# One transformer layer on one core: parts stored one by one, K's and Q's later parts at other places in a chunk, a third score bank in the last chunks

## The reference

```
x = L0_attn_hidden_states                       # (4, 512, 512) float32
x = x + attn(layernorm(x), w_attn, b_attn, w_proj, b_proj)
x = x + ffn(layernorm(x), w_gate, w_up, w_down)

attn: qkv = h @ w_attn + b_attn                 # 32 heads of 16
      scores = q k^T / 16 + slope[h] * (j - i)  # causal
      out = softmax(scores) v;  out @ w_proj + b_proj
ffn:  (silu(h w_gate^T) * (h w_up^T)) w_down^T  # inner width 1376
```

## Time and profile before

| | |
|---|---|
| median of 3 runs | 832.5 us (829.67 to 833.55) |
| the profiled execution | 831.38 us, of which the span is 829.7 |
| PE busy | 782.1 us, 94% |
| DVE, ACT, POOL busy | 643.4, 417.5, 298.7 us |
| mean granted clock of PE | 0.996 |

### The profile page before, as it was taken

The page is one execution under the profiler, slowest core; times in us unless marked ns, Lnnn a source line. Parts: engine busy times, 40 slices in busy tenths (PEclk is TensorE's granted clock), DMA queues, the critical chain, the costliest instruction groups (busy, mean ns, idle before and its releaser), DMA issues.

```text
span 829.7 us, 13389 instructions
## 1 busy us (share of the span) xinstructions
PE 782.1 (94%) x4554; PEld 542.7 (65%) x4554; DVE 643.4 (78%) x1608; ACT 417.5 (50%) x796; POOL 298.7 (36%) x437
## 2 busy tenths in 40 slices
PE   3899899999999999999998899999999999999998
PEld 2655455556555565555554477888878878888886
DVE  6498887878888888977887156849999787888773
ACT  4335666665666566565657524334346434334431
POOL 6223334342443434423434403324441043443342
PEclk9999999999999999999999999999999999999999
DMA  8873656656574565747563416051225321121052
GB/s 285 213 240 111 188 171 197 196 154 204 173 244 140 172 206 181 231 129 218 187 189 130 160 68 217 0 174 43 77 63 179 127 105 66 71 77 52 13 165 101
DMA packets 75372, 122.80 MB, mean 148 GB/s; under 512 B 13075, under 2 KB 38342, under 8 KB 75305
## 3 DMA queue, kind: packets, MB, share of 16 engines
q1 hardware_dynamic: 74217, 121.69, 46.2%
q10 hardware_dynamic: 1088, 0.26, 0.1%
HBM read 79.34 MB, written 42.32 MB: 147 GB/s over the span
## 4 chain that ended last, share of the span: by engine, by line
PE 69%; DVE 13%; DMA 7%; ACT 4%; issue 3%; POOL 2%; SPq 2%; ACTq 0%; DVEq 0%
PE bank L1280 25%; PE bank L1933 12%; PE bank L1199 7%; PE bank L1126 6%; PE bank L1111 5%; PE bank L1182 5%; PE bank L1158 5%; DVE bank L919 4%; DMA pv_dram<-weighed 2%; PE bank L1115 2%; ACT pt L751 2%; POOL scratch L650 1%; DVE scratch L891 1%; DMA row_sums<-pv_dram 1%; DVE mx L917 1%
## 5 line engine op out<-in xcount | busy, mean ns | idle before, releaser
L751 ACT ACTIVATE pt<-bank 128x512 f32<-128x512 f32 (+1 forms) x384 | 196.7, 530 | 124.2 <-PE bank L1182 121.8
L919 DVE CUSTOM_DVE_ANT_0 bank<-bank,mask_qk 128x512 f32<-128x512 f32 (+3 forms) x416 | 195.8, 512 | 42.5 <-PE bank L1158 41.1
L1182 PE MATMUL bank<-q_st,k_st 116*128 116x512 bf16 (+3 forms) x512 | 132.2, 301 | 12.0 <-ACT pt L751 10.6
L1158 PE MATMUL bank<-k_st,q_st 97*128 97x512 bf16 (+3 forms) x512 | 132.8, 306 | 9.5 <-DMA q_st<-slopes_dram 5.4
L1520 POOL TENSOR_TENSOR wd_lo<-wd_raw,wd_hi 128x512 fp32r<-128x512 f32 x34 | 45.7, 1351 | 152.6 <-ACT wd_hi L1552 152.6
L656 POOL TENSOR_SCALAR_AFFINE_SELECT pt<-pt 128x256 f32<-128x256 f32 x128 | 56.1, 438 | 119.8 <-ACT pt L751 119.8
L1158 PEld LDWEIGHTS bank<-k_st,q_st 97*128 97x128 bf16 x512 | 42.0, 98 | 73.2 <-issue 39.5
L660 POOL TENSOR_SCALAR_AFFINE_SELECT pt<-pt 128x256 f32<-128x256 f32 x128 | 54.0, 422 | 78.5 <-ACT pt L751 78.3
L1199 PE MATMUL bank<-pt,v_nat 128*32 128x512 f32 (+3 forms) x1024 | 77.0, 442 | 3.1 <-POOL pt L656 2.3
L1182 PEld LDWEIGHTS bank<-q_st,k_st 116*128 116x128 bf16 x512 | 45.8, 98 | 42.2 <-ACT pt L751 20.7
L1933 PE MATMUL bank<-wd_hi,w_hi 128*128 128x512 f32 x176 | 69.8, 397 | 2.1 <-issue 1.9
(11 more groups left out here) (186 smaller groups left out, 1712.0 us busy)
## 6 DMA issues: line engine op xcount, KB each, us to landing
stack_dram<-scratch SPq DMA_DIRECT2D x32, 384.0 KB, 3.1
q_st<-stack_dram SPq DMA_DIRECT2D x32, 384.0 KB
k_st<-stack_dram SPq DMA_DIRECT2D x32, 384.0 KB
wd_raw<-w_down SPq DMA_DIRECT2D x44, 256.0 KB, 3.4
xt<-w_gate_up SPq DMA_DIRECT2D x20, 512.0 KB, 3.6
stack_dram<-scratch SPq DMA_DIRECT2D x32, 256.0 KB, 3.7
pv_dram<-weighed SPq DMA_DIRECT2D x32, 256.0 KB, 4.5
weighed<-pv_dram SPq DMA_DIRECT2D x17, 256.0 KB
```

The costliest lines, as they stand in the source:

```text
L751: act.activation(pt[:, h % PT_RING, COL0[k]:COL0[k] + WIDE[k]], bank[3 + (3 * h + k) % 2][:, 0:WIDE[k]], ACT.Exp, scale=1.0 / HD).then_inc ...
L919: last = dve.tensor_tensor_reduce(bank[k][:, at:at + n], bank[k][:, at:at + n], mask_qk[:, S - n:S], 1.0, NEG, ALU.add, ALU.max, mx[:, h % ...
L1158: last = pe.matmul(bank[k][:, at:at + n], q_st[0:K_MAX, s, h % 4, t * P:(t + 1) * P], k_st[0:K_MAX, s, h % 4, 0:n], start=True, stop=not b ...
L1182: last = pe.matmul(bank[3 + u % 2][:, at:at + n], k_st[0:K_EXP, s, h % 4, t * P:(t + 1) * P], q_st[0:K_EXP, s, h % 4, t * P:S], start=True ...
```

## The change: part by part

1. `store_parts` issues one DMA as each part is made, each broadcast to the rows that use it (3, 2 and 1 rows; the six rows stand in another order), and waits for `act_read`, `p2_done` and `p3_done` in turn.
2. `load_stacks` issues the slopes' DMA first, ahead of the waits for the stored parts.
3. In SP's loop `store_pv` and the load of the row sums go ahead of the stores of K, except in cb 5.
4. On ACT `second_part` of Q goes behind the second exponential of the last head, and an `attention_hi` of that place behind the third. `second_part` of K moves from head 0 to head 1, except in cb 5; there DVE takes K's remainder ahead of the chunk's first scores.
5. On POOL `clear_future` is cut in two, and a third part goes between its two masks: Q's at head 3, K's at head 1 (in cb 5 ahead of head 0).
6. `weigh_values` waits for the last second mask ahead of its third pass, not its second.
7. From head 114 on the shifted scores use three banks in turn (5, 3, 4).
8. The twelve projection matmuls of chunks 30 and 31 are laid two by two over heads 1 to 3, and all of `weight_lo` is in chunk 30.

```diff
@@ -33,5 +33,4 @@
 
-Q_TERM = (0, 1, 2, 0, 1, 0)
-K_TERM = (0, 0, 0, 1, 1, 2)
-TERMS = len(Q_TERM)
+PART_ROWS = ((slice(2, 5), slice(1, 6, 4), slice(0, 1)), (slice(0, 3), slice(3, 6, 2), slice(4, 5)))
+TERMS = 6
 ROW_X = TERMS * HD
@@ -129,2 +128,10 @@
 
+THREE_FROM = 3 * (HEADS - 14)
+
+
+def shifted_bank(u):
+
+    return 3 + u % 2 if u < THREE_FROM else (5, 3, 4)[(u - THREE_FROM) % 3]
+
+
 def masked_by_tensor(h):
@@ -415,2 +422,6 @@
 
+        def k_at(c):
+
+            return 0 if c % CB == 5 else 1
+
         def late(c):
@@ -494,8 +505,11 @@
                 c, n = "QK".index(kind), group_made(b, g)
-                q_parts, k_parts = part[:, 0, :, :], part[:, 1, :, :]
-                sources = ((q_parts[:, 0:3, :], q_parts[:, 0:2, :], q_parts[:, 0:1, :]),
-                           [k_parts[:, i:i + 1, :].broadcast_to([P, m, S]) for i, m in enumerate((3, 2, 1))])
-                sp.wait_ge(p3_done, 2 * n + c + 1)
-                for r, m, src in zip((0, 3, 5), (3, 2, 1), sources[c]):
-                    sp.dma_start(stack_dram[c, b * G + g, r:r + m].rearrange("r p s -> p r s"), src).then_inc(parts_stored[c], 16)
+                for i in range(3):
+                    if i == 0:
+                        sp.wait_ge(act_read, act_reads(kind, b, g))
+                    if i == 1:
+                        sp.wait_ge(p2_done, 2 * n + c + 1)
+                    if i == 2:
+                        sp.wait_ge(p3_done, 2 * n + c + 1)
+                    sp.dma_start(stack_dram[c, b * G + g, PART_ROWS[c][i]].rearrange("r p s -> p r s"),
+                                 part[:, c, i:i + 1, :].broadcast_to([P, 3 - i, S])).then_inc(parts_stored[c], 16)
 
@@ -505,2 +519,4 @@
                 n = group_made(a // G, a % G)
+                h = 4 * c % H
+                sp.dma_start(q_st[ROW_X:K_SUM:2, s, :, :], slopes_dram[:, h:h + 4, :]).then_inc(stacked[s], 16)
                 for i, st in enumerate((q_st, k_st)):
@@ -509,4 +525,2 @@
                                  [:, at:at + 4, :]).then_inc(stacked[s], 16)
-                h = 4 * c % H
-                sp.dma_start(q_st[ROW_X:K_SUM:2, s, :, :], slopes_dram[:, h:h + 4, :]).then_inc(stacked[s], 16)
 
@@ -577,2 +591,6 @@
                     load_group(loaded_at(c))
+                if c > 0 and cb != 5:
+                    store_pv(c - 1)
+                if sums_of(c) is not None:
+                    load_row_sums(sums_of(c))
                 for kind, mb, i in made(c - 1)[1:]:
@@ -582,6 +600,4 @@
                     load_stacks(c + 3)
-                if c > 0:
+                if cb == 5:
                     store_pv(c - 1)
-                if sums_of(c) is not None:
-                    load_row_sums(sums_of(c))
                 if cb == 3 and b > 0:
@@ -651,3 +667,3 @@
 
-            def clear_future(h):
+            def clear_first(h):
                 head = pt[:, h % PT_RING, :]
@@ -657,2 +673,5 @@
                                    pattern=[[0, 2], [1, P]], channel_multiplier=-1).then_inc(masked, 1)
+
+            def clear_second(h):
+                head = pt[:, h % PT_RING, :]
                 pool.wait_ge(exp_done, 3 * h + 3)
@@ -682,7 +701,8 @@
                 for i in range(4):
-                    if i == 3:
-                        for kind, mb, g in made(c)[:1]:
-                            if kind == "Q":
+                    if i == 0 and k_at(c) == 0:
+                        for kind, mb, g in made(c - 1)[1:]:
+                            if kind == "K":
                                 third_part(kind, mb, g)
-                    if i == 0:
+                    clear_first(4 * c + i)
+                    if i == 1 and k_at(c) == 1:
                         for kind, mb, g in made(c - 1)[1:]:
@@ -690,3 +710,7 @@
                                 third_part(kind, mb, g)
-                    clear_future(4 * c + i)
+                    if i == 3:
+                        for kind, mb, g in made(c)[:1]:
+                            if kind == "Q":
+                                third_part(kind, mb, g)
+                    clear_second(4 * c + i)
                     if i == 3 and statistics_at(c) is not None:
@@ -750,3 +774,3 @@
                 act.wait_ge(t_done, 3 * h + k + 1)
-                act.activation(pt[:, h % PT_RING, COL0[k]:COL0[k] + WIDE[k]], bank[3 + (3 * h + k) % 2][:, 0:WIDE[k]],
+                act.activation(pt[:, h % PT_RING, COL0[k]:COL0[k] + WIDE[k]], bank[shifted_bank(3 * h + k)][:, 0:WIDE[k]],
                                ACT.Exp, scale=1.0 / HD).then_inc(exp_done, 1)
@@ -815,2 +839,4 @@
                     exponential(h, 0)
+                    exponential(h, 1)
+                    held = False
                     if i == 3:
@@ -819,4 +845,4 @@
                                 second_part(*tile)
-                    exponential(h, 1)
-                    if i == 0:
+                                held = True
+                    if i == k_at(c):
                         for tile in made(c - 1)[1:]:
@@ -824,5 +850,7 @@
                                 second_part(*tile)
-                    if highs(c, i) is not None:
+                    if highs(c, i) is not None and not held:
                         attention_hi(*highs(c, i))
                     exponential(h, 2)
+                    if highs(c, i) is not None and held:
+                        attention_hi(*highs(c, i))
                     if tokens_at(c, i) is not None:
@@ -1017,2 +1045,5 @@
 
+                    if i == 0 and k_at(c) == 0:
+                        for tile in made(c - 1)[1:]:
+                            read_tile(*tile)
                     scored(0)
@@ -1032,3 +1063,3 @@
                         for tile in made(c - 1)[1:]:
-                            if (tile[0], tile[2]) != ("P", 3):
+                            if k_at(c) == 1 and (tile[0], tile[2]) != ("P", 3):
                                 read_tile(*tile)
@@ -1054,4 +1085,5 @@
                         normalise_tokens(normalised_at(c), i)
-                    if c in (CHUNKS - 3, CHUNKS - 2):
-                        weight_lo(2 * (c - CHUNKS + 3) + i // 2, i % 2)
+                    if c == CHUNKS - 2:
+                        weight_lo(i, 0)
+                        weight_lo(i, 1)
 
@@ -1135,3 +1167,3 @@
                     k = c - (CHUNKS - 2)
-                    for p in range(lo, min(hi, 3 * TT)):
+                    for p in range(lo // 2, hi // 2):
                         project("P", B - 1, p // 3, 3 * k + p % 3, 3 * k + p % 3 + 1)
@@ -1177,3 +1209,5 @@
                 u = 3 * h + k
-                need(pe, exp_done, u - 1)
+                if u == THREE_FROM:
+                    pe.wait_ge(dve_read, dve_reads("P", B - 2, 2))
+                need(pe, exp_done, u - 1 if u < THREE_FROM else u - 2)
                 for t in T_TILES[k][::-1]:
@@ -1181,3 +1215,3 @@
                     at = S - P if t == 3 else 0
-                    last = pe.matmul(bank[3 + u % 2][:, at:at + n], k_st[0:K_EXP, s, h % 4, t * P:(t + 1) * P],
+                    last = pe.matmul(bank[shifted_bank(u)][:, at:at + n], k_st[0:K_EXP, s, h % 4, t * P:(t + 1) * P],
                                      q_st[0:K_EXP, s, h % 4, t * P:S], start=True, stop=True)
@@ -1192,3 +1226,3 @@
                         pe.wait_ge(m_copied, min(c + 2, CHUNKS))
-                    if t == 1:
+                    if t == 3:
                         pe.wait_ge(masked, 8 * c + 8)
```

6 lines of the change are left out of this document (3 added, 3 removed).

## The result

The changed kernel takes 812.39 us in the median of 6 runs (811.54 to 816.73), the kernel before 831.28 in the same set of runs (6 runs, 827.98 to 833.55): ratio 0.977, 95% interval 0.973 to 0.980. The forecast was 812, in a range of 804 to 824. A later set of runs gave 812.6 and a ratio of 0.974 (0.970 to 0.978). The size is right. Not all of its terms are, and the runs show that the parts of the gain depend on each other in a way that I had not written.

A forecast was written before the change was run, and what follows sets the result against it. PE was taken to bound the kernel, busy for 782.1 us of the span. 831.4 - 13 (middle) - 3 (ahead of the chunks) - 4 (tail) = 811.4; the median lies 1.1 above that execution, so 812, range 804 to 824.

The forecast's parts named there:

- Prologue, 3 us: Ahead of the chunks: stores issued as parts are made, slopes first, shorten PE's first wait; 3 us, bounds 1.3 and 4.4.
- Middle, 13 us: Q/K chunks: the new order removes PE's waits, 1.0 us at each of 13 chunks; bounds 6.5 and 17.8.
- The 1.37 us a Q/K chunk: Time each of a batch's four Q/K chunks was said to lose beyond PE's own pace, about 1.37 us.
- DVE as a brake on chunk 13: Chunk 13: DVE, busy 14.02 of 14.58 us, delays Q's remainder; of the 2 us lost there, 1.0 was left.
- costs nothing: Q/K chunks: K's second part a head later was said to cost nothing while ACT has idle time.
- counted above: SP's order: storing weighed values ahead of K's stores removes DVE's 2.22 us wait, already included in the 13 us.
- thin value: Chunk 13: early stores land K's stack 2 us earlier against a wait of 0.74; cover thin, as PE comes earlier too.
- The late wait: In weigh_values at Q/K chunk ends: waiting for the second mask before the third pass is covered, 0.6 us to spare.
- Tail, 4 us: Last chunks, 29 to 31: third bank, spread projections and moved weight_lo gain 4 us; bounds 1 and 6.
- DVE takes over: Rival: waits for ACT become waits for DVE's maxima or remainder, half the middle term stays; 820 us, chance 0.2.
- Slower: Rival: the last second mask comes too late behind Q's third part and weigh_values stops halfway; 838 us, chance 0.03.
- The clock: Rival: PE's clock falls in the last chunks, the tail gives 1 us or nothing; 815 to 816 us, chance 0.1.

The follow-up runs named there:

- the maxima first: Changed kernel plus one wait: in chunk 29 SP issues the two division loads only after the small DMA of chunk 30's maxima has landed; 812.7 us, ratio 0.979.
- the tail undone: Changed kernel with two score banks to the end, projection matmuls in blocks of four, and weight_lo in chunks 29 and 30 as before; 815.7 us, ratio 0.978.

## Why the prediction was right, and where it was not

**Prologue, 3 us: nothing.** The step that failed is the time that the last store needs to land. The last store does leave 0.03 us behind the third part instead of 0.96. But it took 4.3 to 5.75 us to land in the ten traces with the new order, 3.35 to 5.3 in the four with the old one; my bounds were 3.1 and 4.5. From the end of the third part to the landing that is 5.0 us on average against 5.3. I had called the time to land "not shown with so little ahead of it", but little lies ahead of it only in SP's order: in the changed kernel's trace the two stores ahead of it, issued at 25.87 and 26.99, land at 30.13 and 31.82, and the DMA engines are full from 22.5 to 28.2 us (a share of 1.06). The weights have no part in this; in each trace they had all landed before the first store of parts left. The 2.0 us that the prediction took from the Trainium skill ("DMA: Bandwidth & Descriptors", section "Anatomy of one DMA") stand there for DMAs that GpSimd issues. These come from SP, and none of the 14 landed in under 3.35 us. PE still waits 2.10 us, and the clock still falls (0.73 over the stretch of the earlier trace rows). Chunk 0 started at 52.5 to 55.8 us in the first group and at 51.9 to 55.6 in the second: the third part itself ends anywhere from 27.2 to 30.3 us, so a gain of 0.3 can't be seen.

**Middle, 13 us: 16.4.** The mechanism at the end of a Q/K chunk is as I read it from the earlier trace rows: the last heads of cb 1 and 7 took 3.68 us and now take 2.98, and Q's order undone brings the 3.68 back. (The 1.37 us a Q/K chunk was a mean; by the prediction's own numbers it is 5.3 / 4 = 1.32. The last head of cb 4 gains only 0.18, those of cb 5 up to 1.39.) DVE as a brake on chunk 13 was the mis-sized term: I left it 1.0 us of 2. It took 0.3 in the first trace and nothing in the second, though DVE is full, and chunks 5 and 21 reach 12.53 as well. With that, batches 1 and 2 gained 4.4 us each for my 4.0; batch 0 gained 5.7, 0.85 of it in chunk 3, a chunk with P and T where I had counted none.

**What carries it** I had wrong, and that the total came near is in part luck. I put the 13 us on Q's order, wrote that K's part a head later "costs nothing", that SP's order was "counted above", and gave the early stores thin value. Undone one by one, these four (Q's order, K's place, SP's order, the stores) are worth 11.7, 5.4, 5.7 and 9.7 us: 32.5 for a gain of 16.4. Q's order without the other three makes the middle 6.6 us longer than before (380.4 us); the other three without it gain 4.2 (369.6). Both of these kernels also have the rows' places and the slopes' early DMA. I had the rows for it: each time I measured a DMA against PE as it then ran (a wait of 0.74 us; the earlier trace rows), and did not move the deadline by the 1.37 us a Q/K chunk that I was about to give PE. K's place was the same fault: ACT had idle time over a chunk, but the part stands ahead of the copy on which the transpose one head later depends, and ACT's idle time was in waiting for DVE's remainder ahead of it.

**The late wait** I had costed within the 13 us. It is worth 0.4 to 0.6 us there, and some 0.6 to 1.0 in the last chunk, where I had not counted it.

**Tail, 4 us: 1.8 in one trace, 3.8 in the other.** Over the twelve traces with the new tail it is 3.1 to 4.2 in the nine whose clock stayed up, and 1.6 to 2.4 in the three whose clock fell. Of the 3.8, 0.4 fell in chunk 28, where I had nothing, 0.6 in chunk 29, where I had 1.3 (with the maxima first it was 1.2), and 2.8 in chunks 30 and 31, where I had 3.6 less 0.9 for the clock. In the first trace chunk 29 lost 0.3, and the last two won 1.6. With three banks the clock is 1.00 in every chunk of the tail of the second trace; with two, in the run with the tail undone, it is 0.88, 0.96 and 0.88 in chunks 29 to 31. The Trainium skill ("TensorE: Matmul & The Clock Gate", section "A second HAM failure mode: psum-queue depth-cycling") describes a kernel whose clock swings as it cycles through PSUM banks, and by that the third bank would have brought nothing. The traces do not agree with it here, as far as three edits undone together can tell.

**Rivals.** "DVE takes over": PE waits for DVE's maxima 1.1 us in all. "Slower" by a late second mask: no wait for POOL in the middle. "The clock", which I gave 0.1: it fell in the tail in three of twelve traces, with a gain of 1.6 to 2.4 us left. The one that I did not write is that the DMAs take over as soon as PE runs faster. That is what the runs with SP's order, the stores, or three edits undone show; with K's place alone undone it is mainly ACT's copy.

So the sum by the first traces was 17.5 us for my 20: 3 missing ahead of the chunks, 3.4 more in the middle, 2.8 less from chunk 28 on. Errors of both signs made the total good. The medians of the two kernels in the first set lie 18.9 apart, and that of before came out 1.2 below the one that I started from.

## What to carry to other kernels

When an edit makes the bottleneck engine faster, subtract its gain from the slack of every chain that runs beside it (stores, reloads, row sums, small DMAs), before calling any of them hidden; here one such gain was lost until three other edits moved those chains. An edit "off the path" is to be judged by the instruction queued behind it and by who waits for that, not by the engine's idle time over a chunk. Leaving out one edit at a time misleads here: the parts summed to twice the whole, and only the run with one part alone told why. A wait that one trace shows need not cost what it seems to: look at what the next stretch gains back, in several traces.

## What the runs showed that I had not expected

A small DMA's landing depends on what another engine has issued ahead of it. The 8 KB of the maxima, issued by ACT, took 1.86 or 1.87 us in the four traces where SP's two loads came behind it, 3.64 to 5.12 us in the eight where both had been issued in the 1.7 us ahead of it, and 6.45 us behind six transfers of SP's. The landing of the last store ahead of the chunks (128 KB of parts) scatters from 4.3 to 5.75 us in ten traces with the same order of stores; no run shows why. Once PE had waited 2.06 us, its granted clock was 0.68 over the next 5.4 us, and the 32 matmuls of `weigh_values` took 3.85 us instead of 2.36. In another kernel the clock stayed at 1.00 behind a wait of 1.38 us.
